# Four down chunks spread among the gate and up chunks of a tile

## What is computed

```
first mixture, for each expert:   hidden = silu(x @ wg.T) * (x @ wu.T);   out += weight * (hidden @ wd.T)
second mixture, for each expert:  hidden = relu(x @ w_fc.T) ** 2;         out += weight * (hidden @ w_proj.T)
second mixture, shared expert:    the same with weight 1 for every token
```

## Time and profile before

| | |
|---|---|
| median of 3 runs | 1121.53 us (1119.92 to 1121.6) |
| the profiled execution | 1121.68 us, span 1119.9 us |
| TensorE matmul (PE) | busy 926.1 us, 83% |
| TensorE weight load (PEld) | busy 848.2 us, 76% |
| ScalarE (ACT) | busy 772.2 us, 69% |
| VectorE (DVE) | busy 769.4 us, 69% |
| GpSimd (POOL) | busy 542.8 us, 48% |
| mean granted TensorE clock | 0.928 of full speed |

### The profile page before, as it was taken

How to read it: one execution, slowest core, us unless ns; L and a number is a source line. 1 busy time by engine, 2 the same in 40 slices (tenths; PEclk the granted TensorE clock), 3 DMA queues, 4 the chain that set the end, 5 groups by cost and what they waited for, 6 DMA issues and landing times. The chain is left out here.

```text
span 1119.9 us, 31020 instructions
## 1 busy us (share of the span) xinstructions
PE 926.1 (83%) x11628; PEld 848.2 (76%) x11628; DVE 769.4 (69%) x1496; ACT 772.2 (69%) x1276; POOL 542.8 (48%) x481
## 2 busy tenths in 40 slices
PE   3889999999999999999999742999988569899940
PEld 2788988889889888888889732887868458889830
DVE  6699988988998899889989751422349768410202
ACT  5689988988898889988988441433356166587731
POOL 5376755765656557656655136302318253043423
PEclk8799999999999999999999955999998779899975
DMA  8300000000000000000000043112101002023211
GB/s 267 92 2 21 2 2 21 2 2 20 2 20 3 2 20 2 2 21 2 2 21 3 10 170 97 46 54 61 47 25 31 8 25 69 11 61 95 62 51 42
DMA packets 42254, 41.89 MB, mean 37 GB/s; under 512 B 5505, under 2 KB 37249, under 8 KB 41729
## 3 DMA queue, kind: packets, MB, share of 16 engines
q1 hardware_dynamic: 38016, 31.51, 9.3%
q0 software_dynamic: 4096, 8.40, 2.6%
HBM read 25.60 MB, written 14.29 MB: 36 GB/s over the span
## 5 line engine op out<-in xcount | busy, mean ns | idle before, releaser
L645 DVE TENSOR_TENSOR Pl<-Pr 128x1024 f16<-128x1024 f32 x256 | 325.5, 1293 | 45.8 <-ACT Pr L548 44.4
L548 ACT ACTIVATE Pr<-SC,cur_nesc,cur_esc 128x1024 f32<-128x1024 f32 x256 | 308.8, 1209 | 28.6 <-issue 10.4
L409 PE MATMUL SC<-QK 128*128 128x256 f16 x1024 | 238.9, 274 | 1.0 <-ACT QK L530 1.0
L410 PE MATMUL SC<-QK 128*128 128x256 f16 x1024 | 238.9, 274 | 0.0
L435 PE MATMUL OP<-V,Pr 128*128 128x129 f16 x2048 | 212.0, 220 | 9.4 <-DVE osum L666 9.4
L437 PE MATMUL OP<-V,Pl 128*128 128x65 f16 x2048 | 205.3, 192 | 0.0
L435 PEld LDWEIGHTS OP<-V,Pr 128*128 128x128 bf16 x2048 | 183.9, 97 | 16.4 <-issue 13.6
L757 POOL TENSOR_TENSOR Ob<-osum,rden 128x128 f32<-128x128 f32 x128 | 133.4, 1042 | 109.7 <-DVE osum L666 109.0
L437 PEld LDWEIGHTS OP<-V,Pl 128*128 128x128 f16 x2048 | 180.9, 97 | 2.7
L1663 POOL DMA_INDIRECT yg<-ys,slots x64 | 74.8, 1169 | 145.7 <-DMA ys<-yb 63.0
L1161 PE MATMUL DB<-wd,hid 128*128 (+1 forms) x864 | 125.9, 290 | 12.1 <-DVE x L1495 6.7
(11 more groups left out here) (189 smaller groups left out, 2083.2 us busy)
## 6 DMA issues: line engine op xcount, KB each, us to landing
ys<-yb SPq DMA_DIRECT2D x92, 64.0 KB
xg<-xs SPq DMA_DIRECT2D x12, 384.0 KB, 4.5
wst<-in_up SPq DMA_DIRECT2D x8, 512.0 KB
xs<-zero SPq DMA_DIRECT2D x2, 1472.0 KB
scratch<-in_up SPq DMA_DIRECT2D x1, 2304.0 KB, 8.6
wd<-in_wd SPq DMA_DIRECT2D x1, 2304.0 KB, 13.7
wd<-in_wd SPq DMA_DIRECT2D x1, 2048.0 KB
QK<-in_wqkv SPq DMA_DIRECT2D x4, 384.0 KB, 7.3
```

What stands on the lines that cost most here:

```text
L409: eng.matmul(out, QK[:, b, 1, key:key + P], rhs, start=True, stop=False)
L410: mm = eng.matmul(out, QK[:, b, 2, key:key + P], rhs, start=False, stop=True)
L548: eng.activation(Pr[:, n % PB, :, :], SC[s % 2][:, :, :], ACT.Exp, bias=cur_nesc[:, b:b + 1], scale=cur_esc[:, b:b + 1]).then_inc(s_exps, 1)
L645: eng.tensor_tensor(Pl[:, n % PB, :, :].rearrange("p a b -> p (a b)"), pr, high(pr)[:, 1::2], ALU.subtract).then_inc(s_low_probs, 1)
```

## The change

TensorE's down products of tile u - 2 are no longer issued as one group behind all products of tile u. In the first mixture chunks 0 and 1 stand behind gate chunks 1 and 3, and chunks 2 and 3 behind up chunks 1 and 3. In the second mixture, which has no up chunks, chunk 0 stands behind gate chunk 1, chunk 1 behind gate chunk 2, chunks 2 and 3 behind gate chunk 3. The waits ahead of the down products move with chunk 0. The semaphore for finished gate products is still raised by the last gate product. The other engines' orders are as they were.

```diff
+DOWN_BY_GATE = (((), (0,), (), (1,)), ((), (0,), (1,), (2, 3)))
+DOWN_BY_UP = ((), (2,), (), (3,))
...
-            def up_products(u):
+            def up_products(u, behind=None):
...
-                    mm = eng.matmul(o, wl[:, at], xh, start=False, stop=True)
-                mm.then_inc(s_gate_products, 1)
+                    gate = eng.matmul(o, wl[:, at], xh, start=False, stop=True)
+                    if c == NC - 1:
+                        gate.then_inc(s_gate_products, 1)
+                    if behind is not None:
+                        for part in DOWN_BY_GATE[l][c]:
+                            down_part(behind, part)
...
-                    mm.then_inc(s_up_products, 1)
+                        if c == NC - 1:
+                            mm.then_inc(s_up_products, 1)
+                        if behind is not None:
+                            for part in DOWN_BY_UP[c]:
+                                down_part(behind, part)
...
+            def down_part(u, c):
...
+                if c == 0:
+                    if l == 0:
+                        eng.wait_ge(s_hidden, u + 1)
+                    else:
+                        wait(eng, s_squared, u + 1 - 2 * TILES)
...
+                    wait(eng, s_down_read, sorted_before(u))
+                    wait(eng, s_shared_added, shared_before(u))
+                mm = eng.matmul(DB[:, 0:D], hid[:, u % HR, P * c:P * c + P], wd[l][:, bass.ds(first + P * c, P)],
+                                start=c == 0, stop=c == NC - 1)
+                if c == NC - 1:
+                    mm.then_inc(s_down_products, 1)
...
-                    up_products(u)
-                if u >= LAG2:
+                    up_products(u, u - LAG2 if u >= LAG2 else None)
+                else:
                     down_products(u - LAG2)
```

More of the change, by code:

```diff
@@ L1143, in up_products @@
                         mm = eng.matmul(o, wl[:, at], xh, start=False, stop=True)
-                    mm.then_inc(s_up_products, 1)
-            def down_products(u):
+                        if c == NC - 1:
[4 more added lines that the diff above has]
+            def down_part(u, c):
                 if sorted_tile(u):
@@ L1150, in down_products @@
                     l, first = 1, E * FF
[L1151 to L1159, removed]
+                if c == 0:
[3 more added lines that the diff above has]
+                        wait(eng, s_squared, u + 1 - 2 * TILES)
+                    if u == SHARED_0:
+                        eng.wait_ge(s_wd1_loaded, 16)
+                    wait(eng, s_down_read, sorted_before(u))
[4 more added lines that the diff above has]
+                    mm.then_inc(s_down_products, 1)
+            def down_products(u):
                 for c in range(NC):
-                    mm = eng.matmul(DB[:, 0:D], hid[:, u % HR, P * c:P * c + P],
-                                    wd[l][:, bass.ds(first + P * c, P)], start=c == 0, stop=c == NC - 1)
-                mm.then_inc(s_down_products, 1)
+                    down_part(u, c)
             def step_products(b):
@@ L1211, in _ @@
                 if u < SPARSE_2:
-                    up_products(u)
-                if u >= SHARED_0 + LAG2:
+                    up_products(u, u - LAG2 if u >= SHARED_0 + LAG2 else None)
+                else:
                     down_products(u - LAG2)
@@ L1225, in _ @@
                 if u < UNITS:
-                    up_products(u)
-                if u >= SPARSE_2 + LAG2:
+                    up_products(u, u - LAG2 if u >= SPARSE_2 + LAG2 else None)
+                else:
                     down_products(u - LAG2)
```

## The result

| | before | after |
|---|---|---|
| median | 1120.98 us (4 runs) | 1168.36 us (4 runs, 1166.9 to 1169.37) |
| profiled span | 1119.9 us | 1166.3 us |
| TensorE matmul busy | 926.1 us | 938.8 us |
| ScalarE busy | 772.2 us | 772.6 us |
| mean granted clock | 0.928 | 0.93 |

Ratio 1.0423, 95% interval 1.0405 to 1.0441: slower by 47.4 us. The forecast was 1162.6 in a range of 1150 to 1176. Both traces have 11628 matmul records, and ScalarE's busy time has not changed. TensorE's records add up to 12.7 us more; what is added is in the main waiting.

The account below looks back on a forecast made before the run. TensorE lines lead the chain of waits, with ScalarE the pace in second-mixture sorted tiles. Terms 1.8 + 1.1 + 12.7 + 13.5 + 6.1 + 3.5 + 2.2 = 40.9 us on 1121.68 gave 1162.6 us, range 1150 to 1176.

Parts of the forecast that it names:

- Step (b): First down chunk's wait for DB now stands inside the gate, closing a ring through ScalarE in the second mixture.
- The ring of the second mixture: Closed chain of waits, relu to copy of DB to TensorE's gate to relu: 2.74 us a tile, for 1.83.
- Shared tiles: Tiles 80 to 84: chain of waits over VectorE's add, 2.07 us a tile, 10.4 for five.
- Step (a): Switching TensorE from f16 to f32 products costs 0.05 each, 0.15 or 0.10 a tile: 0 to 13 us.
- the term "first mixture": First-mixture tiles wait for ScalarE's copy of DB: about 32 tiles x 0.11, +3.5 us (0 to 6).
- The ring: In the first mixture: last down pass, copy, down and f16 chunks sum to 2.83, taken as 2.86, for 2.74 to 2.76.
- the stretch 57 to 60: Tiles 58 and 59 lose 1.8 us; two down chunks inside the gate cost 0.55 each at 57 and 60.
- Tiles 77 to 88: Chains of waits over ScalarE, then VectorE's add: 27.9 us together, for 21.75, +6.1; tile 85 at 2.4.
- A: Rival: spreading fills the array's holes in the first mixture, faster, about 1115 us; chance 0.03.
- B: Rival: the wait for DB isn't met, only switching costs, 2 to 6 us, 1123 to 1128; chance 0.06.
- C: Rival: TensorE's recurring idle times lower its clock to 1.2 GHz in about 48 tiles, 1206 us; chance 0.06.
- D: Rival: the change does nothing because of unseen slack, 1121.5 us; chance 0.02.

Follow-up runs that it names:

- e3: Changed kernel with ScalarE's copy of DB moved between relu and square in the second mixture, TensorE's order untouched: 1142.64 us, ratio 1.0211 to the kernel before.
- e4: Changed kernel with second-mixture down chunk 0 behind gate chunk 2 and the other three behind gate chunk 3: 1145.15 us, ratio 1.0233 to the kernel before.
- e5: Changed kernel with two banks for the down products, except one bank in tiles 41 to 59: 1126.59 us, ratio 1.0066 to the kernel before.
- e6: Kernel before the change, down products in one group, given two banks for them: 1113.44 us, ratio 0.9949 to the kernel before.
- e7: Changed kernel, one bank, first-mixture chunks spread from gate chunk 3 over up chunks 0 to 2, second mixture grouped: 1119.41 us, ratio 0.9995 to before.
- e1: Changed kernel with down chunks spread in the first mixture only, second mixture grouped again: 1125.71 us, ratio 1.0053 to the kernel before.
- e2: Changed kernel with down chunks spread in the second mixture only, first mixture grouped again: 1159.07 us, ratio 1.0361 to the kernel before.
- e8: Changed kernel with two banks for the down products, spread in the first mixture only, second grouped: 1114.61 us, ratio 0.9952 to the kernel before.

## Why the prediction was right

*Direction and mechanism.* Step (b) held: e3 and e4 change single links of the ring and move it as its sum says, and e5 against e6 puts at least 34 of the 47.4 us down to the wait for DB. The price of spreading that is left with two banks is 13.2 us.

*The ring of the second mixture*: 2.74 forecast, 2.75 measured; stretches 60 to 76 and 88 to 106 gave 12.8 and 14.3 for 12.7 and 13.5. Shared tiles: 2.07 forecast, 2.05 measured. TensorE's idle time about 0.7, measured 0.70.

*Step (a)*: 0.05 per switch, shown where the array is the limit (e5, 1.73 for 1.63 in the shared tiles and 1.83 for 1.73 in the sorted ones of the second mixture), hidden in the first mixture (e7).

*What was too small.* The whole is 5.8 us over the forecast. The largest part is the term "first mixture": +3.5 forecast, 7.2 between tiles 2 and 44. Some of this is scatter between executions. Over the same stretch the traces of e1, e3 and e4, whose first mixture is the same, took 133.6 for 135.4, and that of e2, whose first mixture is grouped, 126.9 for 128.2; e1's median gives 6.75. So the term came out at about twice its size.

The ring was forecast at 2.83 and taken at 2.86 with pauses; it measured 2.98 (median, copy to copy). Averaged over the 30 tiles of the earlier trace rows's stretch that load no offsets, its parts are these. From the copy's end to the first down pass it took 0.25, not the 0.18 that I carried over from the second mixture (731.24 + 0.28 to 731.75 is one of 0.23). The rounds of two f16 chunks and a down chunk took 0.64, not 0.61 (732.44 to 733.10 is one of 0.66). The first chunk with its two f16 chunks took 0.66 for 0.67, so that part was right, and the last chunk and the turn to the copy 0.03 more than forecast. In the rounds the array and the queue's register operations run nearly level (five operations, 0.60 us, against 0.61), so a pause in the queue that the lead over a group of four down chunks used to cover can hold the array up. That the pauses are the reason is read from the trace, not tested.

Next is the stretch 57 to 60, 3.4 for 2.35. Tiles 58 and 59 took 2.75 each as forecast; tile 60 took 1.5 more, where 0.55 was forecast for the two down chunks inside its gate. That price is one at full clock. From tile 60's transposes to the end of its gate the windows show (busy per engine, then PEclk), before and then after:

```profile
976.88:978.33 1.45, 1.45 (x15) 1.45 (x16) 1.23 (x16) 0.39 (x1) 0.00 (x0) 0.50 0.02 6
```

```profile
988.20:990.71 2.51, 2.51 (x19) 2.39 (x20) 2.22 (x27) 0.38 (x1) 0.00 (x0) 0.50 0.01 3
```

The granted clock is 0.50 in both, and the two chunks cost 1.06, twice the 0.55. Tiles 77 to 88 took 28.25 for 27.9, and the error is in tile 85: the prediction took 2.4 for it, though the trace of before already has 2.76 there; it measured 2.94.

*The rivals.* A: e7 and e8, nothing gained. B: TensorE did have to wait, except where the wait was moved (e7) or opened (e5). With it open, B's price of 2 to 6 us for the switches is borne out (5.7, e5 against e6 in tiles 60 to 106). C: the granted clock stayed at 1.00 with 0.70 us idle in each tile from 88 to 106, so short idle times alone did not bring it down here. The Trainium skill, TensorE: Matmul & The Clock Gate, section "A second HAM failure mode: psum-queue depth-cycling", tells of a kernel in which frequent short idle times between groups of matmuls made the clock go up and down; this trace does not agree. D is out.

## What to carry to other kernels

When work is moved ahead in an in-order queue, its waits move too, and everything that is now behind them gets a new condition: follow each wait to its releaser, see what stands in front of the releaser on its own engine, and whether that in turn needs something now behind the wait. If it does, the ring's sum is the new pace, and one timeline of before can give it: to 0.01 us in the second mixture here, but 0.12 to 0.15 short in the first, where one link had been carried over from the other mixture. A single accumulator bank can make such a ring; a second bank opened this one and gave 6 us without any spreading. To price what an edit costs with the ring open, compare with the old kernel that has the second bank too.

## What was not expected of the hardware

A wait of TensorE's queue is recorded in two ways. In a sorted tile of the second mixture the record covers the waiting (1022 ns). In the first mixture the records are all 51 ns (six from 730.7 to 737.5) although TensorE's first down pass follows the copy's end in each tile; the one ahead of it starts at 731.55, 0.04 behind the copy's end, and the waiting shows only as a gap ahead of the record. The rows of the first mixture, then those of a shared tile:

```profile
L34 PEldq EVENT_SEMAPHORE  x6: 51/51/51, 730.7 to 737.5; - x6
...
L34 PEldq EVENT_SEMAPHORE  x2: 51/51/51, 1048.5 to 1048.6; - x2
```

The number of semaphores does not decide. By the operands in the trace the instruction names one semaphore in the first mixture (the copies) and two in the second (VectorE's adds, then the copies). The shared tile has the two as well, and TensorE waits there for the add, which ends at 1048.41; yet the record is 51 ns and starts 0.04 behind it. What fits all 30 of these records from 1002 to 1080 us is the place in the instruction: a record starts when the semaphore named first has been reached and covers only the wait for the second. No kernel was made to test this. A queue's waiting time can't be summed from these records alone.
